# Seven tiles a layer gathered by rows from SyncE, count stores on ACT, first indices loaded alone, and the last output blocks in halves and partly on GpSimd

## The reference

```
h = x
for l in range(2):                                   # relational layers
    W = einsum('rb,bio->rio', coeff[l], basis[l])
    msg = einsum('ni,rio->rno', h, W)[etype, src] * norm
    h = segment_sum(msg, dst) + bias[l]              # ReLU after the first
x = layernorm(x + h)
h = x @ W_in + b_in
for l in range(3):                                   # mean layers
    agg = segment_sum(h[src], dst) / deg
    h = relu(agg @ W_agg[l] + h @ W_self[l] + b_hid[l])
x = layernorm(x + h @ W_out + b_out)
```

## Time and profile before

| | us |
|---|---|
| median of 3 runs | 1949.28 |
| lowest, highest | 1945.72, 1952.35 |
| the profiled execution | 1949.9 |
| its span in the trace | 1947.7 |

### The profile page before, as it was taken

How to read it: one execution, slowest core, us unless ns; L and a number is a source line. 1 busy time by engine, 2 the same in 40 slices (tenths; PEclk the granted TensorE clock), 3 DMA queues, 4 the chain that set the end, 5 groups by cost and what they waited for, 6 DMA issues and landing times.

```text
span 1947.7 us, 32221 instructions
## 1 busy us (share of the span) xinstructions
PE 1658.1 (85%) x9643; PEld 1378.4 (71%) x9643; DVE 1180.2 (61%) x4040; ACT 477.0 (24%) x1016; POOL 1236.8 (63%) x1302
## 2 busy tenths in 40 slices
PE   5787888778777777887889888888999999999997
PEld 4676666666666666676677777777777887777776
DVE  7978755656656656566676767775445664322355
ACT  2001111111111111121222222222546212533332
POOL 6777777777777777777777777777777775000000
PEclk9889899899999999999999999999999999999999
DMA  9334444444444444344444444444555442210011
GB/s 260 104 111 117 114 115 115 119 115 115 119 116 116 115 119 115 109 126 125 137 125 126 130 130 125 123 138 136 157 160 161 125 131 76 78 49 1 9 41 48
DMA packets 144637, 221.63 MB, mean 114 GB/s; under 512 B 79518, under 2 KB 99886, under 8 KB 144462
## 3 DMA queue, kind: packets, MB, share of 16 engines
q0 software_dynamic: 62016, 169.04, 30.9%
q1 hardware_dynamic: 77454, 45.63, 8.3%
q10 hardware_dynamic: 4992, 4.88, 0.8%
HBM read 202.30 MB, written 17.13 MB: 113 GB/s over the span
## 4 chain that ended last, share of the span: by engine, by line
PE 51%; DMA 33%; POOL 7%; issue 4%; DVE 3%; ACT 1%; DVEq 0%; ACTq 0%
PE bank L981 21%; DMA RY<-in_x,si 20%; DMA RY<-H,di 13%; PE bank L1206 9%; PE bank L840 8%; POOL RY L330 7%; PE bank L890 2%; PE bank L1172 2%; PE bank L1216 2%; PE bank L823 1%; PE bank L1261 1%; PE bank L905 1%; PE bank L807 1%; PE bank L863 1%; PE bank L822 0%
## 5 line engine op out<-in xcount | busy, mean ns | idle before, releaser
L981 PE MATMUL bank<-RY 128*128 128x128 f32 x5160 | 778.9, 292 | 244.1 <-DMA RY<-in_x,si 155.4
L981 PEld LDWEIGHTS bank<-RY 128*128 128x128 f32 x5160 | 688.2, 199 | 350.2 <-DMA RY<-in_x,si 199.9
L330 POOL DMA_INDIRECT RY<-in_x,si x645 | 617.7, 958 | 200.8 <-issue 137.1
L330 POOL DMA_INDIRECT RY<-H,di x630 | 599.9, 952 | 192.0 <-issue 142.3
L600 DVE TENSOR_SCALAR RY<-iot,c,wgt 128x128 f32<-128x128 f32 x1290 | 454.2, 357 | 401.9 <-PE bank L981 400.3
L681 ACT CAST RY<-bank 128x320 uint8<-128x320 f32 x215 | 91.5, 425 | 729.6 <-PE bank L823 725.6
L478 DVE TENSOR_SCALAR RY<-iotN,bcol 128x320 bf16<-128x320 f16 x645 | 213.1, 330 | 0.0
L1206 PE MATMUL bank<-Ar,hs 125*128 125x500 f32 x800 | 204.2, 405 | 0.0
L592 DVE TENSOR_TENSOR RY<-RY,bank 128x256 f32 x430 | 178.5, 415 | 24.7 <-issue 15.0
L840 PE MATMUL bank<-RX,RY 128*128 128x256 f32 x704 | 189.8, 399 | 1.0 <-issue 0.6
L840 PE MATMUL bank<-RY 128*128 128x256 f32 x704 | 181.7, 384 | 2.4 <-DVE RY L592 2.2
(11 more groups left out here) (141 smaller groups left out, 1226.9 us busy)
## 6 DMA issues: line engine op xcount, KB each, us to landing
RY<-in_x,si POOLq DMA_INDIRECT x645, 2.8
RY<-H,di POOLq DMA_INDIRECT x630, 2.8
Ad<-RY SPq DMA_DIRECT2D x215, 40.0 KB
A<-Ad SPq DMA_DIRECT2D x22, 312.5 KB, 3.3
D<-Ad SPq DMA_DIRECT2D x20, 305.2 KB
RX<-in_basis ACTq DMA_DIRECT2D x2, 2048.0 KB, 20.8
AhG<-Ad SPq DMA_DIRECT2D x6, 610.4 KB
H<-RY SPq DMA_DIRECT2D x22, 128.0 KB
```

The source lines that it names most:

```text
L330: e.indirect_dma_start(G[0:k, n % NG, :], None, table, bass.IndirectOffsetOnAxis(ap=index[0:k, t:t + 1], axis=0)).then_inc(s_land[n % NG], 16)
L981: mm = e.matmul(bank[2 + wg % 3][:, c * 128:(c + 1) * 128], G[0:k, n % NG, c * 128:(c + 1) * 128], S[0:k, n % NSS, :], start=(i == 0 and n ...
```

## The change

- *Rows.* Tiles 96, 180, ..., 600 (84 apart) of each layer are no longer gathered by GpSimd. SyncE issues one DMA of 1 KB for each of their 128 rows, from the table seen as bytes, at a byte offset in a register; eight offsets are loaded per call, without a bounds check. The rows of a tile are spread over the 84 tiles that end 12 tiles before its own. They land in two slots GS. The slots of G go by a tile's place among the gathered ones.
- *Their indices* come as a new input of 2 x 512 numbers, loaded by SyncE once zeros have been written to the last rows of H1 and waited for; DVE multiplies them by 1024 at tile 20.
- The row of zeros of H1 moves from row 0 to row 2500, so the indices of layer 1 need no shift; the indices of the first 15 gathers are worked out in one step more.
- *Count stores* move from SyncE's queue to ACT's, behind the conversion.
- *Indices of the first 16 tiles* are loaded by a DMA of their own ahead of the others.
- *Window 20 of layer 0*: its ten steps stand at tiles 631 to 636 where they stood at 632 to 638.
- *End.* The output of block 15 moves behind the last chunk. Mean and ReLU of the last chunk are made in halves of 250 columns, and the outputs of blocks 16 and 17 need the first half only. GpSimd adds all 20 biases and does the norms of blocks 16, 17 and 18. The stores of blocks 18 and 19 are two DMAs each, of 112 and 13 rows.

```diff
+ROW_TILES = [96 + 84 * j for j in range(7)]
+ROW_LEAD = 12
+ROW_PARTS = range((len(ROW_TILES) + 3) // 4)
...
-                tile = end + 3 + 2 * k // 3 if l == 0 and g == NW - 2 else first + by * k
+                tile = end + 2 + (k + 1) // 2 if l == 0 and g == NW - 2 else first + by * k
...
+def row_plan():
+
+    plan = {}
+    for j, tile in enumerate(ROW_TILES):
+        lo, hi = (ROW_TILES[j - 1] - ROW_LEAD if j else 2), tile - ROW_LEAD
+        for r in range(128):
+            plan.setdefault(lo + r * (hi - lo) // 128, []).append((j, r))
+    return plan
...
+ROWS = row_plan()
+
+POOLED = [n for n in range(2 * T) if n % T not in ROW_TILES]
+PLACE = {n: p for p, n in enumerate(POOLED)}
+
+POOL_NORM = (16, 17, 18)
...
-    H1z = dram("H1", (N + 1, D))
-    H1 = H1z[1:N + 1, :]
+    H1 = dram("H1", (N + 1, D))
...
+        GS = ei[:, 0:512].bitcast(F32).rearrange("p (s f) -> p s f", f=256)
+        GS8 = ei[:, 0:512].bitcast(U8).rearrange("p (s f) -> p s f", f=4 * D)
...
-            e.dma_start(si[:, :], srcT).then_inc(s_src, 16)
+            e.dma_start(si[:, 0:FIRST], srcT[:, 0:FIRST]).then_inc(s_src0, 16)
+            e.dma_start(si[:, FIRST:T], srcT[:, FIRST:T]).then_inc(s_src, 16)
...
-            e.indirect_dma_start(G[0:k, n % NG, :], None, table, bass.IndirectOffsetOnAxis(ap=index[0:k, t:t + 1], axis=0)).then_inc(
-                s_land[n % NG], 16)
+            e.indirect_dma_start(G[0:k, slot, :], None, table, bass.IndirectOffsetOnAxis(ap=index[0:k, t:t + 1], axis=0)).then_inc(
+                s_land[slot], 16)
...
-            for n in range(FIRST, 2 * T):
-                if n >= NG:
-                    e.wait_ge(s_sum, n - NG + 1)
+            e.wait_ge(s_src, 16)
+            for p in range(FIRST, len(POOLED)):
+                n = POOLED[p]
+                e.wait_ge(s_sum, POOLED[p - NG] + 1)
                 if n == T:
                     e.wait_ge(s_fixi, 4)
                     e.wait_ge(s_zrow, 32)
                     e.wait_ge(s_h1, 16 * (NW - 1))
                 if n == T + FIX:
                     e.wait_ge(s_h1, 16 * NW)
-                rows_of(e, n, x if n < T else H1z[0:LOW + 1, :] if n < T + FIX else H1z, si if n < T else siF if n < T + FIX else si1)
+                rows_of(e, n, x if n < T else H1, siF if T <= n < T + FIX else si)
...
+            for j in range(JB - 1):
+                pool_bias(e, j)
+            pool_norm(e, 16)
+            pool_bias(e, JB - 1)
+            pool_norm(e, 17)
+            pool_norm(e, 18)
...
+                if l == 0 and t == 20:
+                    e.wait_ge(s_ix, 16 * len(ROW_PARTS))
+                    at = di[0:32 * len(ROW_PARTS) - 31, 0:512]
+                    e.tensor_scalar(at, at, 4 * D, None, ALU.mult).then_inc(s_at, 1)
...
+            if w == 0:
+                e.wait_ge(s_prep, 40)
+            r = row_base(e, ba2i[0:1, w:w + 1], 8 * (N - 1))
             if w >= 4:
                 e.wait_ge(s_ad, 16 * (w - 3))
             e.wait_ge(s_cnt, a + 1)
             e.copy(Aw8[:, w % 4, :], bank[6 + w % 2][:, 0:NB]).then_inc(s_aw8, 1)
+            if w > 0:
+                e.wait_ge(s_ad, 16 * w)
+            e.wait_ge(s_aw8, w + 1)
+            e.dma_start(Adw[bass.ds(r, 128), :], Aw8[:, w % 4, :]).then_inc(s_ad, 16)
...
+                    if n in PLACE:
+                        rows = G[0:k, PLACE[n] % NG, c * 128:(c + 1) * 128]
+                        if c == 0:
+                            e.wait_ge(s_land[PLACE[n] % NG], 16 * (PLACE[n] // NG + 1))
+                    else:
+                        q = row_number(l, n - l * T)
+                        rows = GS[:, q % 2, c * 128:(c + 1) * 128]
+                        if c == 0:
+                            e.wait_ge(s_row[q % 2], 16 * 128 * (q // 2 + 1))
...
+        def sp_zero_rows(e):
+
+            e.wait_ge(s_zero, 2)
+            e.dma_start(H1[LOW:N, :], h1w[:, 0, :]).then_inc(s_zrow, 16)
+            e.dma_start(H1[N:N + 1, :], h1w[0:1, 0, :]).then_inc(s_zrow, 16)
+            e.wait_ge(s_zrow, 32)
+
+        def sp_indices(e):
+
+            for i in ROW_PARTS:
+                e.dma_start(di[32 * i:32 * i + 1, 0:512], src_rows[i:i + 1, :]).then_inc(s_ix, 16)
+
+        def bytes_of(table):
+            return table.bitcast(U8).rearrange("(o n) f -> o (n f)", o=1)
+
+        def sp_rows(e, l, t):
+
+            table = bytes_of(x if l == 0 else H1)
+            for j, r in ROWS.get(t, []):
+                q = l * len(ROW_TILES) + j
+                if l == 0 and j + r == 0:
+                    e.wait_ge(s_at, 1)
+                if l == 1 and j + r == 0:
+                    e.wait_ge(s_h1, 16 * NW)
+                if r == 0 and q > 1:
+                    e.wait_ge(s_sum, (q - 2) // len(ROW_TILES) * T + ROW_TILES[(q - 2) % len(ROW_TILES)] + 1)
+                if r % 8 == 0:
+                    half, at = divmod(j * 128 + r, 512)
+                    _, regs[:] = nc.values_load_multi_w_load_instructions(
+                        di[32 * half:32 * half + 1, at:at + 8], engines=[mybir.EngineType.SP], min_val=0, max_val=(N - 1) * 4 * D,
+                        skip_runtime_bounds_check_because="indices are numbers of rows of the table")
+                e.dma_start(GS8[r:r + 1, q % 2, :], table[0:1, bass.ds(regs[r % 8], 4 * D)]).then_inc(s_row[q % 2], 16)
+
+        regs = []
 
         def sp_layer(e, l):
             if l == 0:
-                sp_zero_row(e)
+                sp_zero_rows(e)
+                sp_indices(e)
...
+                sp_rows(e, l, t)
...
+        def dve_last_mean(e):
+
+            e.wait_ge(s_relu, 2 * (3 * NC - 2))
+            e.wait_ge(s_agg, 2 * NC * JB)
+            for half in range(2):
+                a, b = half * 2 * PB, half * 2 * PB + 2 * PB
+                for mo in range(2):
+                    e.scalar_tensor_tensor(agT[:, 1, mo, a:b], degb[:, N - CH + a:N - CH + b], bT[:, 6 + mo:7 + mo],
+                                           bank[2 + mo][:, a:b], ALU.mult, ALU.add).then_inc(s_mean, 1)
+
+        def act_last_combine(e):
+            for half in range(2):
+                a, b = half * 2 * PB, half * 2 * PB + 2 * PB
+                for mo in range(2):
+                    e.wait_ge(s_mean, 2 * (2 * NC - 1) + 2 * half + mo + 1)
+                    e.activation(hT[:, mo, N - CH + a:N - CH + b], agT[:, 1, mo, a:b], ACT.Relu).then_inc(s_relu, 1)
...
-            e.wait_ge(s_relu, 2 * (2 * NC + j // 4 + 1))
+            e.wait_ge(s_relu, 2 * (2 * NC + j // 4 + 1) + (2 if j >= JB - 2 else 0))
...
+            if j in POOL_NORM:
+                return
...
+        def pool_norm(e, j):
+            s = j % 4
+            e.wait_ge(s_od[s], 16 * (j // 4))
+            e.wait_ge(s_rec, NW + j + 1)
+            e.tensor_scalar(ob[0:PB, s, :], yb[0:PB, s, :], sm[0:PB, s, 0:1], sm[0:PB, s, 3:4], ALU.subtract,
+                            ALU.mult).then_inc(s_po, 1)
...
+                e.wait_ge(s_po, POOL_NORM.index(j) + 1)
+            else:
+                e.wait_ge(s_o, j + 1 if j < POOL_NORM[0] else j + 1 - len(POOL_NORM))
+            for a, b in ((0, PB),) if j < JB - 2 else ((0, 112), (112, PB)):
+                e.dma_start(out[j * PB + a:j * PB + b, :], ob[a:b, j % 4, :]).then_inc(s_od[j % 4], 16)
...
-            if l < 2 or c == 0 or i < 0:
+            if l < 2 or c == 0 or i < 0 or (c == NC - 1 and i > 8):
...
-            for j in range(JB - 4, JB):
+            for j in range(JB - 5, JB):
```

More of the change, by code:

```diff
@@ L147, in take, with program @@
     e.sem_clear(sem)
-def program(nc, x, ramp, ramp_col, srcT, dstT, etT, wT, large, small, basis, coeff, bias, W_in, b_in, W_agg, W_self,
+def program(nc, x, ramp, ramp_col, src_rows, srcT, dstT, etT, wT, large, small, basis, coeff, bias, W_in, b_in, W_agg, W_self,
             b_rows, W_out, b_out, out):
@@ L297, in program @@
         s_bias, s_out, s_y = sem("s_bias"), sem("s_outp"), sem("s_y")
-        s_o, s_od = sem("s_o"), [sem(f"s_od{i}") for i in range(4)]
+        s_o, s_po, s_od = sem("s_o"), sem("s_po"), [sem(f"s_od{i}") for i in range(4)]
         (k_start, k_own, k_ix, k_rows, k_prod, k_z, k_x, k_tr, k_ht, k_mm, k_cp, k_row, k_st, k_back, k_y, k_bn, k_sq, k_gather, k_xd, k_md) = (
@@ L606, in dve_fix_indices @@
             e.tensor_scalar(srcB, sf[:, 0:FIX], float(-LOW), None, ALU.add).then_inc(s_fixi, 1)
-            e.tensor_scalar(si1, sf, 1.0, None, ALU.add).then_inc(s_fixi, 1)
             e.wait_ge(s_fixi, 1)
-            e.scalar_tensor_tensor(siF, sf[:, 0:FIX], 1.0, lowm, ALU.add, ALU.mult).then_inc(s_fixi, 1)
+            e.scalar_tensor_tensor(idxf, sf[:, 0:FIX], float(-N), lowm, ALU.add, ALU.mult).then_inc(s_fixi, 1)
+            e.wait_ge(s_fixi, 3)
+            e.tensor_scalar(siF, idxf, float(N), None, ALU.add).then_inc(s_fixi, 1)
         def dve_layer(e, l):
@@ L1394, in act_mean_layers @@
                         convert(e, n, True)
-            act_combine(e, 2, NC - 1)
-            for j in range(JB - 4, JB):
+            act_last_combine(e)
```

(19 more changed lines are left out.)

50 lines of the change are left out of this document (18 added, 32 removed).

## The result

The changed kernel takes 1935.03 us (median of 6 runs, 1931.23 to 1937.55), the kernel before beside it 1949.18: a ratio of 0.9931, 95% interval 0.9920 to 0.9942, 13.5 us faster. The forecast was 1927, 22 us faster. A second series (e9) gave 0.9921 (0.9908 to 0.9934). The profiled execution took 1937.55 us with a span of 1935.5; the profiled one of before took 1949.9 with 1947.7.

A forecast was written before the change was run, and what follows sets the result against it. GpSimd's gather issue, one per 1.25 us, was taken as the bound up to tile 536 of layer two. 16.3 + 1.3 + 1.1 + 3.4 = 22.1 us off 1949.9 gave 1927.8, taken as 1927; own range 1922 to 1933, wider 1921 to 1936.

The forecast's parts named there:

- the rival that the second layer gives less: Second layer: D loads, ACT conversions and TensorE set the pace, so tiles 432 and 516 gain nothing; 1933 us, 14%.
- Fourteen tiles: Both layers' gathers: each tile off GpSimd before tile 536 of layer two saves 1.25 us; 16.3 us in all.
- SyncE's rows hidden: SyncE's queue: row DMAs at 0.52 us each stay hidden, with room up to 0.79 and 0.73 us by layer.
- No difference: Rival on the gathers: added row traffic lengthens each one, 17 ns each eating 22 us; 1949 us, 4%.
- First indices alone: Kernel start: a small separate index load lands sooner for GpSimd's first gather; gain 1.3 us (0 to 1.9).
- Indices and count stores: Row indices loaded after H1's zeros, and count stores moved to ACT: both hidden by slack, cost 0.
- Between the layers: GpSimd's 3.67 us stall between the relational layers shortens by earlier apply steps; gain 1.1 us (0 to 3.4).
- The end: Serial tail and the output moved ahead of it: four parts together save 3.4 us (1.5 to 4.5).
- (a): End: block 15's output leaves the last chunk, four matmul instructions fewer; 0.9 us less.
- (b): End: mean and ReLU before the first output are made by halves; 0.7 us less.
- (d): End: the last stores are divided, landing sooner despite a second issue; 1.0 us less.
- (c): End: DVE's output steps lose two bias adds and three norms to GpSimd; 0.8 us less.

The follow-up runs named there:

- e9: The changed kernel run again without any edit, beside the other runs on one chip: 1934.36 us, ratio 0.9921.
- e8: The changed kernel with tiles by rows in the first layer only, the second layer's seven gathered by GpSimd again: 1942.08 us, ratio 0.9959.
- e4: The changed kernel with no tiles gathered by rows and their index arithmetic on VectorE left out: 1944.99 us, ratio 0.9988.
- e1: The changed kernel with the norms of blocks 16, 17 and 18 back on VectorE, biases still on GpSimd: 1928.67 us, ratio 0.9902.
- e2: As e1, with the 20 bias additions back on VectorE too: 1928.69 us, ratio 0.9904.
- e10: The changed kernel with all 1792 row transfers made but unused, GpSimd gathering all tiles itself: 1944.50 us, ratio 0.9987.
- e11: As e2, with eight tiles a layer by rows, every 62nd from 96 to 530: 1926.22 us, ratio 0.9890.
- e5: As e2, with ten tiles a layer by rows instead of seven, every 49th from 96 to 537: 1958.82 us, ratio 1.0042.
- e3: The kernel before with a one-column GpSimd memset added that waits for the last norm: ratio 0.9998.
- e13: The changed kernel with 14 unused gathers added on GpSimd behind its casts, norms still on GpSimd: 1930.04 us, ratio 0.9900.

## Why the prediction came out as it did

The time lay in the range given, and the mechanism of the rows was the right one: GpSimd's issues are the bound up to tile 536, and rows on SyncE take them off at no cost that shows. But the gain was 14 us, not 22, and the difference is chiefly one thing that the sum did not have. That the time was still in the range is in part luck. 1935 us lies outside the forecast's own range, 1922 to 1933; only the wider one, 1921 to 1936, holds it, and that was widened for the rival that the second layer gives less, with its 1933 us. By the time alone that rival would have won; e8 shows that it did not happen.

*Fourteen tiles, 16.3 us.* Right: 16.6 us between e4 and e1/e2 and 17 between e10 and e13, within 2 to 4 us. Layer by layer it held too: e8 gave 7.4 us for the second layer against 6 x 1.25 = 7.5. That tile 600 brought nothing follows from the chain, whose last gather (1479.18 us) stands 108 gathers before the last one; no run tests it by itself.

*SyncE's rows hidden.* Right, with 0.43 us a row for 0.52. The DMA instruction took 0.228 us for one row where I had taken 0.332, the price of a store of 128 rows; the 8-register load took 0.79 us where I had taken one register's 0.27, and an eighth of it is small either way. The bound of 0.73 us a row in the second layer was not reached at seven tiles. The same sum for the spacings of e11 and e5 gives, as an estimate, 0.54 us ((61 x 1.25 - 8) / 128) and 0.42 us ((48 x 1.25 - 6) / 128); with some 0.5 us a row beside the D loads it holds at eight tiles and fails at ten, as was seen. What the sum did not have is the price of a row behind a D load, 1.3 to 1.7 us.

*No difference.* e10 settles it: the transfers alone cost 0.0001 +- 0.0013 of the time. The Trainium skill ("DMA: Bandwidth & Descriptors", "Why a DMA increments its semaphore by 16 and not by 1") was weighed in the prediction, which took from it that a row of bytes is cut into 16 pieces of 64 B. The page of the changed kernel and that of e4, SyncE's queue (packets, MB, share):
```profile
q1 hardware_dynamic: 49988, 38.78, 7.0%
```
```profile
q1 hardware_dynamic: 46400, 36.94, 6.5%
```
That is 3588 packets and 1.84 MB more for 1792 rows (and the two small loads of their indices): two packets a row, 1 KB in all, where 16 pieces would have made over 28,000. The measurement decides; these rows were not cut so.

*First indices alone, 1.3 us.* The first gather starts 0.5 to 0.8 us earlier, in all profiles of kernels with this part. The small load landed after 3.4 us, later than the 2.7 us borrowed from SyncE's loads of x; the wait for it is 3.7 to 4.1 us where it was 4.5 and 4.6.

*Indices and count stores, 0.* No run takes these two apart. The last gather of the first layer comes 9.3 us earlier, and seven tiles (8.8) with the earlier start (0.6) make 9.4, so nothing is seen of a cost there.

*Between the layers, 1.1 us.* Not shown. The profile that I predicted from had a stall of 3.67 us; e3, the same code up to there, had 1.95. With the moved steps it was 1.5 to 1.8 in ten profiles, 2.2 in e11 and 3.87 in e13. From e3's 1.95 to the usual 1.5 to 1.8 it is 0.2 to 0.4 us, and two profiles of the old code don't show even that. The 3.67 and 3.87 us, in the old code and in the new, are chance that one profile could not tell.

*The end, 3.4 us less.* This is the step that failed: it came out about 2.5 us longer. Its own parts were near. (a) The stretch of aggregate matmuls is 258.4 us instead of 259.3, as forecast. (b) to (d), 2.5 forecast, gave a tail of 14.7 in e4 (13 to 14 forecast) against 16.1 and 16.8 before, 1.4 to 2.1. Within that, (d) was worth 1.0 to 1.6 (1.0 forecast), and (c), VectorE's relief by GpSimd, nearly nothing: 14.7 and 14.3 with the norms on GpSimd (e4, e13), 14.4 without (e2). I took 0.5 us for GpSimd's norm and it was 1.22, against 0.41 on VectorE; its bias took 0.74, against 0.39 there. The bias of block 19 stood behind norm 16 and ended at 1924.25 us; VectorE's first step for block 19 began at 1924.35, after 1.10 us without work. The term that was missing, so in effect put at nothing, is the drain. Moving GpSimd's last work from 1643 to 1927 us also moved the drain behind it, from a place where it is hidden to the end of the program, and taking gathers off GpSimd made it four times as long. Neither half costs alone: e4 has late work and a short drain, e2 a long drain and early last work. Together they cost 5.1 us (19.4 against 14.3).

In one line: 22.1 forecast, less 5.1 for the drain, about 0.9 between the layers, 0.5 at the start and 0.7 in the rest of the end leaves an estimated 15, and 13.5 and 15.4 were measured in the two series.

## What to carry to other kernels

Work that is moved to an idle engine near the end moves that engine's own end too: look in the trace at what each engine still does behind its last instruction of work, and how long. A queue that takes over many small transfers is bounded where the other transfers behind them stand closest, not by its mean load: with rows in 52% of SyncE's time they cost nothing that showed, and with 90% they cost more than they brought, because six tiles of work took SyncE 8.3 us where 7.5 were to be had. And a stall of 2 us seen in one execution is not a term of a sum until a second profile shows it.

## What was not expected of the hardware

GpSimd's drain at the program's end took 1.5 to 12.3 us. With the same last work (three norms) it was 2.3, 2.3, 2.2 and 3.3 us where GpSimd had made 1288 or 1290 gathers, and 9.7, 9.2 and 9.2 us where it had made 1283 or 1276; with the casts as last work it was 5.5 us at 1290 and 11.9 to 12.3 us at 1270 to 1276. e10 and e13 show that the number of gathers decides, not SyncE's transfers, and that the 14 gathers shorten it in either of two places, inside the layers or behind the casts. Why, and what it does at other numbers, stays open: it may be a limit, or the place in some cycle on which the count ends. 1284 to 1287 were not tried.

A DMA of one 1 KB row costs SyncE 0.228 us of issue against 0.26 to 0.39 for its larger ones, and a load of eight registers from SBUF 0.79 us against 0.27 for one. A row issued directly behind a D load of 305 KB takes 1.3 to 1.7 us in the stretch of e5 shown; what holds it is not shown.

TensorE fell to half its clock between 1480 and 1530 us in every profile, in the two of the changed kernel busy without a gap from 1495 us until then. How long it stayed there differed between these two executions of the same kernel, 10.3 and 6.9 us, and made 1.7 us of the 3.1 between them.
